# The third synapse quarter as two compared planes that TensorE adds up, a guess from three chunks, and one output quarter compared on GpSimd

## What is computed

```python
xn = layernorm(x)
# attention branch: q, k, v = xn @ Wq, Wk, Wv; rotary; linear attention by chunks of 128 with a
# decayed state (8 chunks a sequence); rms norm with rms_w; @ Wo
# network branch:
z = xn @ ternary(W_syn).T + b_syn              # 2048 columns; ternary: round(W / mean|W|), clipped to -1, 0, 1
thresh = top_k(z, 204)[:, -1:]                 # the 204th largest of a row
hidden = where(z >= thresh, relu(z), 0)
out = layernorm(xn + hidden @ ternary(W_out).T + b_out)
result = x + attention(xn) + out
```

## Time and profile before

| what | value |
|---|---|
| median of 3 runs | 953.33 us (952.49 to 953.53) |
| the profiled execution | 952.98 us, its span 951.2 us |
| TensorE busy | 904.9 us, 95% of the span |
| VectorE, ScalarE | 732.2 us and 730.3 us, 77% each |
| GpSimd | 659.0 us, 69% |
| TensorE, slices 1 to 6 of 40, in tenths | 4 8 5 7 9 9, from then on 9 |
| granted clock, slices 1 to 5, in tenths | 9 9 7 7 9, mean 0.984 |

### The profile page before, as it was taken

How to read it: one execution, slowest core, us unless ns; L and a number is a source line. 1 busy time by engine, 2 the same in 40 slices (tenths; PEclk the granted TensorE clock), 3 DMA queues, 4 the chain that set the end, 5 groups by cost and what they waited for, 6 DMA issues and landing times.

```text
span 951.2 us, 22133 instructions
## 1 busy us (share of the span) xinstructions
PE 904.9 (95%) x8307; PEld 443.2 (47%) x8307; DVE 732.2 (77%) x1826; ACT 730.3 (77%) x1322; POOL 659.0 (69%) x588
## 2 busy tenths in 40 slices
PE   4857999999999999999999999999999999999987
PEld 2423544444444444444444444444444444444434
DVE  5869877877777787777778777777787777778775
ACT  6788778887777887777778887777887777779672
POOL 1535688677677767767876776877766767886763
PEclk9977999999999999999999999999999999999999
DMA  9875644444444354543534444444354444444431
GB/s 336 242 199 100 119 81 76 91 100 79 87 93 99 69 91 89 95 85 79 101 80 77 90 101 79 85 95 94 64 98 92 90 87 82 90 84 85 79 66 47
DMA packets 257422, 94.49 MB, mean 99 GB/s; under 512 B 243488, under 2 KB 243744, under 8 KB 256544
## 3 DMA queue, kind: packets, MB, share of 16 engines
q1 hardware_dynamic: 253472, 85.64, 45.4%
q10 hardware_dynamic: 3840, 7.41, 2.2%
HBM read 24.34 MB, written 8.39 MB: 34 GB/s over the span
## 4 chain that ended last, share of the span: by engine, by line
PE 77%; ACT 7%; issue 6%; DVE 3%; DMA 3%; POOL 2%; SPq 1%; DVEq 1%; ACTq 0%; POOLq 0%
PE proj L1108 42%; PE p_ffn L1220 10%; PE p_wo L1267 8%; PE p_ffn L1250 8%; PE rows L1176 3%; PE rows L1166 2%; ACT Pr L647 2%; ACT hl L665 1%; DMA area<-in_L_ffn_W_syn_dram 1%; PE rows L1187 1%; PE rows L1197 1%; DMA area<-in_L_attn_Wk_dram 1%; SPq L275 1%; DVE c L1656 1%; PE p_ffn L1236 1%
## 5 line engine op out<-in xcount | busy, mean ns | idle before, releaser
L1108 PE MATMUL proj<-wqkv,xT 128*128 128x512 f16 x1152 | 261.2, 384 | 1.9 <-ACT area L489 0.7
L1108 PE MATMUL proj<-wsynT,xT 128*128 128x512 f16 x1024 | 246.8, 385 | 5.3 <-DMA wsynT<-xrn 4.0
L907 POOL TENSOR_TENSOR hl<-area,hl 128x2048 f16<-128x2048 f32 x31 | 141.2, 4556 | 98.0 <-ACT hl L665 98.0
L1108 PEld LDWEIGHTS proj<-wqkv,xT 128*128 128x128 f16 x1152 | 111.9, 99 | 135.2 <-ACT area L489 10.9
L1108 PEld LDWEIGHTS proj<-wsynT,xT 128*128 128x128 f16 x1024 | 93.6, 99 | 118.5 <-issue 11.9
L1510 DVE SCALAR_TENSOR_TENSOR area<-proj,c,gb 128x512 f32<-128x512 f32 x128 | 95.4, 746 | 38.4 <-PE proj L1108 36.4
L1220 PE MATMUL p_ffn<-woutT,area 128*128 128x512 f16 x480 | 109.3, 378 | 0.0
L1250 PE MATMUL p_ffn<-woutT,area 128*128 128x512 f16 x480 | 108.7, 379 | 0.0
L1606 DVE MAX8 cand<-area 128x8 f32<-128x128 f32 x512 | 105.2, 277 | 1.1
L1267 PE MATMUL p_wo<-wo,ahl 128*128 128x512 f16 x384 | 90.3, 384 | 1.2 <-ACT ahl L467 0.7
L1682 DVE SCALAR_TENSOR_TENSOR area<-area,c 128x2048 f32<-128x2048 f32 x32 | 75.2, 2350 | 18.7 <-ACT c L552 18.3
(11 more groups left out here) (251 smaller groups left out, 1733.4 us busy)
## 6 DMA issues: line engine op xcount, KB each, us to landing
xrn<-in_L_attn_x_dram SPq DMA_DIRECT2D x32, 256.0 KB, 3.1
out_dram<-pair_b SPq DMA_DIRECT2D x29, 256.0 KB, 2.0
woutT<-in_L_ffn_W_syn_dram ACTq DMA_DIRECT2D x2, 1024.0 KB, 11.1
area<-in_L_ffn_W_syn_dram ACTq DMA_DIRECT2D x2, 1024.0 KB, 11.9
woutT<-in_L_ffn_W_out_dram SPq DMA_DIRECT2D x2, 1024.0 KB, 6.3
area<-in_L_attn_Wq_dram ACTq DMA_DIRECT2D x1, 1024.0 KB, 6.8
area<-in_L_attn_Wk_dram ACTq DMA_DIRECT2D x1, 1024.0 KB, 9.7
area<-in_L_attn_Wv_dram ACTq DMA_DIRECT2D x1, 1024.0 KB, 11.8
```

Source lines behind the costliest of these rows:

```text
L907: nc.gpsimd.tensor_tensor(hl[:, 1, :], src, hl[:, 0, :], ALU.subtract).then_inc(S["lo_ready"], 1)
L1108: last = nc.tensor.matmul(bank, xT[:, b.par, k, :], w, start=m == 0, stop=m == len(pairs) - 1)
```

## The change

Five things move.

- Synapse quarter 2 is still compared twice on VectorE, but no longer subtracted and no longer transposed by DMA: TensorE transposes and adds the two planes (`planes_flipped`) into two banks, in groups 0, 1 behind the second tile's v projection and 2, 3 behind quarter 3's groups, and VectorE casts the four groups (`planes_flat`).
- The first tile's guess is taken from chunks 0, 1 and 3; chunk 2 follows. On GpSimd the scaling of gb goes ahead of the rows of Wo, and the second tile's rotary goes from the first step into the prologue.
- ScalarE sums output quarters 1 and 0 behind the first tile's first two counts, no longer in the prologue; the third count follows them at once, ahead of the output mean.
- Output quarter 3 is compared twice on GpSimd (`out_compared`) behind the output threshold, and subtracted on VectorE (`ternary_of_planes`) at the start of the second step.
- The order around these: the addition of output quarter 2 goes behind the selection; ScalarE's second sign pass of quarter 0 goes into the second step, ahead of the second tile's work; VectorE's row statistics of tile 3 go behind the first three groups of segments; on SP the query and key transposes of tile 1 go between the transposes of output quarters 2 and 3.

```diff
@@ -96,6 @@
+spare = area2[:, 4608:4608 + N // 2].bitcast(F16)
@@ -164,7 @@
-halves_3 = [ahl.rearrange("p a g c -> p (a g c)"), xhl.rearrange("p a n -> p (a n)")]
@@ -173,7 @@
-flips = {1: [sbank[1], sbank[2], p_av, p_ffn], 3: [sbank[1], sbank[2], p_av, p_ffn]}
+flips = {1: [sbank[1], sbank[2], p_av, p_ffn], 3: [sbank[1], sbank[2], p_av, p_ffn],
+         2: [sbank[0], p_wo, sbank[0], p_wo]}
@@ -182,7 @@
-    "synT0", "synT2", "syn_flip", "syn_flat1", "syn_flat3", "x_flip", *(f"outT{q}" for q in range(4)),
+    "synT0", "syn_planes", "syn_flip", "syn_flip2", "syn_flat2", "out_planes", "syn_flat1", "syn_flat3", "x_flip", *(f"outT{q}" for q in range(4)),
@@ -334,7 @@
-        syn_transposed(2, 2)
@@ -346,7 @@
     def out_transpose(q):
-        sp.wait_ge(S[f"out_tern{q}"], 2 if q == 3 else 1)
+        sp.wait_ge(S[f"out_tern{q}"], 1)
@@ -354,7 @@
-            sp.wait_ge(S["out_sign"], 9)
+            sp.wait_ge(S["out_sign"], 6)
@@ -390,12 @@
-            sp.wait_ge(S["out_sign"], 5)
+            sp.wait_ge(S["out_planes"], 2)
...
+            qk_transposed(b)
...
-        if b:
+        elif b:
@@ -462,8 @@
-        if u.n == 0:
-            act.wait_ge(S["out_tern3"], 2)
@@ -560,8 @@
-        if a.n == 3:
-            act.wait_ge(S["out_tern3"], 2)
@@ -610,7 @@
-        sums("out", (2, 3, 1, 0))
+        sums("out", (2, 3))
@@ -661,7 @@
-            act.wait_ge(S["out_sign"], 7)
+            act.wait_ge(S["out_sign"], 4)
@@ -684,21 @@
+        sums("out", (1, 0))
+        third_count(t)
...
-        third_count(t)
...
-        sign("out", out_in[3][:, 0:N // 2], halves_3[0], out_thr[1])
-        wait(act, "xT_ready", Tile(1, 0), 16, 16)
-        sign("out", out_in[3][:, N // 2:N], halves_3[1], out_thr[1])
-        sign("out", out_in[3], out_t[3], out_thr[0])
...
-        act.wait_ge(S["outT2"], 16)
-        sign("out", out_in[0], out_t[0], out_thr[0])
@@ -708,6 @@
+        act.wait_ge(S["outT2"], 16)
+        sign("out", out_in[0], out_t[0], out_thr[0])
@@ -883,17 @@
+        pool.wait_ge(S["rows_loaded"], 16)
+        pool.wait_ge(S["gb_scale"], 1)
+        pool.wait_ge(S["syn_planes"], 2)
+        nc.gpsimd.tensor_scalar(gb, gb, pc[:, 44:45], 1.0, ALU.mult, ALU.mult).then_inc(S["gb_ready"], 1)
...
-        pool.wait_ge(S["rows_loaded"], 16)
-        pool.wait_ge(S["gb_scale"], 1)
-        pool.wait_ge(S["syn_tern"], 2)
-        nc.gpsimd.tensor_scalar(gb, gb, pc[:, 44:45], 1.0, ALU.mult, ALU.mult).then_inc(S["gb_ready"], 1)
...
+        rotary(second)
...
+        rotary_added(second)
@@ -942,6 @@
+    def out_compared(q):
...
+        pool.wait_ge(S["out_thr"], 2)
+        nc.gpsimd.tensor_scalar(out_t[q], out_in[q], out_thr[0], 2.0, ALU.is_gt, ALU.mult).then_inc(S["out_planes"], 1)
+        nc.gpsimd.tensor_scalar(spare, out_in[q], out_thr[1], 2.0, ALU.is_lt, ALU.mult).then_inc(S["out_planes"], 1)
@@ -958,6 @@
+            out_compared(3)
@@ -978,8 @@
-            rotary(b)
-            rotary_added(b)
@@ -1063,6 @@
+    def planes_flipped(groups):
...
+        for g in groups:
+            wait_for(pe, "syn_flat2", g - 1)
+            for k in range(KB):
+                at = slice(g * E + k * P, g * E + (k + 1) * P)
+                for n, plane in enumerate((syn_other[2], syn_t[2])):
+                    pe.wait_ge(S["syn_planes"], n + 1)
+                    last = nc.tensor.matmul(flips[2][g][:, k * P:(k + 1) * P], plane[:, at], ident16,
+                                            start=n == 0, stop=n == 1)
+            last.then_inc(S["syn_flip2"], 1)
@@ -1095,10 @@
-            if n in (3, 5):
-                pe.wait_ge(S[f"synT{n - 3}"], 16)
-            else:
-                pe.wait_ge(S["syn_flat1" if n == 4 else "syn_flat3"], 4)
+            pe.wait_ge(*((S["synT0"], 16), (S["syn_flat1"], 4), (S["syn_flat2"], 4), (S["syn_flat3"], 4))[n - 3])
@@ -1135,8 @@
+        planes_flipped((0, 1))
...
+        planes_flipped((2, 3))
@@ -1398,6 @@
+    def planes(src, high, low, thr):
...
+        nc.vector.tensor_scalar(high, src, thr[0], 2.0, ALU.is_gt, ALU.mult).then_inc(S["syn_planes"], 1)
+        nc.vector.tensor_scalar(low, src, thr[1], -2.0, ALU.is_lt, ALU.mult).then_inc(S["syn_planes"], 1)
@@ -1484,11 @@
-        ternary(syn_in[2], syn_t[2], syn_other[2], syn_thr)
+        planes(syn_in[2], syn_other[2], syn_t[2], syn_thr)
...
+        planes_flat((0, 1))
...
+    def planes_flat(groups):
...
+        for g in groups:
+            dve.wait_ge(S["syn_flip2"], g + 1)
+            nc.vector.tensor_copy(wsynT[:, 8 + g].rearrange("p k t -> p (k t)"),
+                                  flips[2][g]).then_inc(S["syn_flat2"], 1)
@@ -1534,14 @@
-        for n in (0, 1, 3, 2):
+        for n, part in ((0, 0), (1, 1), (3, 2)):
...
+            if n == 0:
+                planes_flat((2, 3))
...
-            then(nc.vector.bn_stats(seed6[:, n, :], z[:, 0, n * 512:(n + 1) * 512]))
-            if n == 3:
-                row_topped(4)
-        then(nc.vector.bn_aggr(pc[:, 50:52], seed6))
+            then(nc.vector.bn_stats(seed6[:, part, :], z[:, 0, n * 512:(n + 1) * 512]))
+        then(nc.vector.bn_aggr(pc[:, 50:52], seed6[:, 0:3, :]))
...
+        row_topped(4)
+        z_chunk(first, 2)
@@ -1564,12 @@
     def ternary_of_signs(q, n):
...
-        if q < 3:
-            nc.vector.tensor_tensor(out_t[q], out_t[q], signs_b, ALU.add).then_inc(S[f"out_tern{q}"], 1)
-        else:
-            for l in range(2):
-                part = out_t[q][:, l * N // 2:(l + 1) * N // 2]
-                nc.vector.tensor_tensor(part, part, halves_3[l], ALU.add).then_inc(S["out_tern3"], 1)
+        nc.vector.tensor_tensor(out_t[q], out_t[q], signs_b, ALU.add).then_inc(S[f"out_tern{q}"], 1)
...
+    def ternary_of_planes(q):
...
+        dve.wait_ge(S["out_planes"], 2)
+        nc.vector.tensor_tensor(out_t[q], out_t[q], spare, ALU.subtract).then_inc(S[f"out_tern{q}"], 1)
@@ -1712,8 @@
+        wo_low()
...
-        wo_low()
@@ -1724,28 @@
-        ternary_of_signs(2, 2)
...
-        ternary_of_signs(3, 5)
...
+        ternary_of_signs(2, 2)
...
     def following_step():
...
-        row_stats(a)
+        ternary_of_planes(3)
...
-        ternary_of_signs(0, 7)
-        row_shift(a)
...
+        ternary_of_signs(0, 4)
...
-        q_decayed(t)
+        row_stats(a)
...
+        q_decayed(t)
...
+        row_shift(a)
@@ -1753,7 @@
-        ternary_of_signs(1, 9)
+        ternary_of_signs(1, 6)
...
```

## The result

The changed kernel takes **962.25 us** in the median of six runs (959.72 to 962.91) where the kernel before, beside it, takes 953.28 us (952.03 to 955.55). The ratio is 1.0082 [1.0068, 1.0096]: 9.0 us slower, where 2.5 us faster was forecast, and above the range. The profiled execution took 962.53 us, its span 960.7 us.

The account below looks back on a forecast made before the run. The start of TensorE's second-tile values was taken to bound the kernel: second guess 7.1 us earlier, 4.2 given back by the new order, 0.4 by TensorE's clock, leaving 2.5 us: 953.33 to 950.8 us, range 947.9 to 953.9 us.

Parts of the forecast that it names:

- Part 4, the two comparisons: GpSimd's two new comparisons of output quarter 3: 1.99 us each, 4.0 us in all, taken from a multiplication's row.
- The far bound: Upper end for the cost of one GpSimd comparison: L907 with its two inputs, 4.56 us on the mean.
- Part 4, no slack behind them: GpSimd's squares behind the comparisons come just when the second tile's guess needs them; every further microsecond of comparing costs one.
- the mark: Moment TensorE starts the second tile's values, 104.02 us before, forecast near 101.3 us; only bringing it forward shortens the run.
- Rival 3: Slower: GpSimd's comparisons cost what L907 does, 9.1 us, 5.1 more, giving 955.9 us; chance 0.06.
- Parts 1 and 2: Synapse quarter transposed on TensorE and first guess from three chunks: first guess at 53.2 us, 6.6 us earlier.
- Part 3: Two ScalarE sums behind the counts: third count ends at 65.25 us, 3.9 us earlier, with VectorE idling 2 us.
- Second guess at the price taken: With comparisons at 1.99 us each, the second tile's guess comes at 79.0 us, 7.1 us earlier.
- Part 5, the gate of the row statistics: GpSimd's L907 waits for tile 3's late row statistics and their power; the new order gives back 4.2 of 7.1 us.
- Rival 1: GpSimd starts L907 when ScalarE's high half is there, not held by statistics: 3.2 us more stay, 947.6 us; chance 0.08.
- Part 5, TensorE's clock: TensorE at half speed after idling some 3.5 us before GpSimd's low half: 0.4 us lost, bounds 0 and 1.1.
- The sum by the mark: The run shortens by what the mark gains: 2.9 less 0.4, so 2.5 us, giving 950.8 us on the median.

Follow-up runs that it names:

- e1: Changed kernel with both GpSimd comparisons of output quarter 3 turned into multiplications of the same form, shape and types; 954.79 us, ratio 1.0001 to the kernel before.
- e5: Changed kernel with five more one-input GpSimd operations ahead of the two comparisons, each ended before the next, to time the forms alone; one run, 981.08 us.
- e2: Changed kernel with only the first of the two GpSimd comparisons, the quarter subtracted from itself; 955.57 us, ratio 1.0023 to the kernel before.
- e7: e4 with the sums of output quarters 1 and 0 back in ScalarE's prologue, ahead of the first guess; 950.82 us, ratio 0.9965 to the kernel before.
- e4: e3 with GpSimd's power for tile 3 moved behind the low halves in its second step; 950.31 us, ratio 0.9955 to the kernel before.
- e3: Changed kernel with output quarter 3's two planes made by ScalarE sign passes and added on VectorE; 952.78 us, ratio 0.9982 to the kernel before.

## Why the prediction was wrong

- **Part 4, the two comparisons: the step that failed.** "I take 1.99 each", from L893, a multiplication of the same form. Measured: 7.17 us each, 10.35 us more in all. The far bound, L907's 4.56 us, was no bound: it is another operation again, with two inputs but plain arithmetic. e1 and e5 show that the shape and form were right and the operation was what counted. The rule of the Trainium skill that was weighed there (GPSIMD Engine Reference, Performance pitfalls for Q7 kernels) pointed the right way: an estimate of 3.5 us from its 2.03 cycles an element for a body that compares and selects. The runs show twice that for `tensor_scalar`, and also for a maximum.
- **Part 4, no slack behind them: held.** e2 shows 0.4 us of slack, and in e5 20.3 us of GpSimd's work delay the guess by 20.3 us. Of the 9.6 us by which the mark comes later than in e1, 8.7 us are there at the second guess, the rest is TensorE's clock ahead of the mark.
- **Rival 3, slower: the right mechanism and place**, with its point of decision at 4.2 us a comparison. It was priced at 4.56 us and given 0.06, and its 955.9 us lay outside the stated range, which ended at 953.9 us. With 7.17 us in it, its own working gives 950.8 + 10.35 = 961.2 us; measured, 962.25 us.
- **Parts 1 and 2: held.** First guess at 53.2 us forecast, 53.0 to 53.8 us in all kernels with both parts. TensorE's sixteen matmuls end at 49.81 us (49.3 forecast).
- **Part 3: the times held, its worth isn't shown.** Third count done at 65.46 us (65.25 forecast), VectorE idle 2.04 us (2 forecast); without it (e7) the kernel takes the same time within what can be told.
- **Second guess at the price taken: held.** 79.0 us forecast, 79.61 us in e1. VectorE's own queue took 1.35 us ahead of it, where it took 0.64 us in the kernels before and after; what makes the difference stays open.
- **Part 5, the gate of the row statistics: held, and shown by e4.** The last probability was forecast to end at 101.1 us and ends at 101.14 us in e1. That it fits so closely is in part luck: the guess was 0.6 us late, and the way from the settled guess 0.6 us shorter than forecast. Rival 1 said what it is worth without the gate, 3.2 us more; e4 starts the subtraction 3.3 us earlier beyond its earlier guess, and has the mark 3.55 us earlier, of which 0.7 us is again the earlier guess.
- **Part 5, TensorE's clock: the second term mis-sized.** 0.4 us taken, between 0 and 1.1. The twelve matmuls behind the idle 3.69 us took 1.42 and 3.24 us in e1, against 1.04 us (four) and 1.89 us (eight) at full speed: 1.7 us lost. In the kernel after they took 5.2 us from start to mark, 2.5 us lost. The bound took half of 2.6 us, but twelve matmuls take some 2.8 us at full speed, and half speed adds as much again. So even with cheap comparisons the mark would have moved by e1's 0.9 us, not by the forecast 2.5 us, and e1's medians show no gain that can be told.
- **The sum by the mark: held.** Over all eight kernels timed against the kernel before, the shift of the mark (+8.7, -0.9, +0.8, -0.5, -4.1, -1.0, -3.0, -0.1 us in the table's order) and the difference of the medians (+9.0, +0.4, +1.1, -1.7, -4.1, -2.5, -3.1, -1.0 us) agree within 1.5 us.

## What to carry to other kernels

A duration may be carried from one row to another only for the same operation: the same GpSimd form over the same columns took 1.97 us as a sum or product and 7.17 us as a comparison or maximum, and the row with the longest time in the trace was no upper bound. When work goes to an engine that is busy 69% of the time, ask what stands behind it in that engine's order and who waits for that; here it was a sum of squares for the next guess, with 0.4 us of slack. When a gain vanishes between two marks, look for a small operation that stands ahead of a large one on an in-order queue: moving 0.56 us of power behind 5.3 us of low halves was worth 2.5 us (952.78 to 950.31 us).

## What the runs showed of the hardware

- GpSimd's `tensor_scalar` on 128 rows of float32: is_gt, is_lt or max with a product, float16 out, takes 7.17 us for 2048 columns; is_gt alone 5.45 us; a sum or product with a product 1.97 us. For is_gt with a product, 512, 1024 and 2048 columns lie on 3.4 ns a column and some 0.3 us.
- VectorE beside it: the selection's L1729, 128x32 with two inputs in SBUF, takes 0.84 us in e3 and 4.27 us beside the comparison. It ends at 78.05 us, 2.5 us before the comparison does; in e5, beside the maximum that ran from 71.40 to 78.57 us, it ends at 76.02 us, again 2.5 us before. Beside L903, L1541 ends 0.6 us after it (106.40 and 105.84 us). The Trainium skill (SBUF — State Buffer, SBUF: two separate sides) has the port pair that the two engines share locked for the whole instruction. L903 agrees. The comparison and the maximum don't: VectorE's operation was over when a good third of their time was still to come.
- TensorE's granted clock: behind 3.69 us of idling it was 0.50, its lower level, in the kernel after (107.4 to 112.8 us) and in e1 (100.2 to 102.0 us), as it was 0.50 in the kernel before behind 4.05 us (52 to 56 us). In e4, behind 2.10 us of idling, it was 0.50 from 102.0 to 103.2 us, and eight matmuls took 3.04 instead of 1.90 us. In e7, behind 2.11 us at the same place, it was 1.00 throughout (102.0 to 105.0 us), and the same eight took 1.90 us. So the length of the idle time alone doesn't decide it.
